# One table set for logarithm and exponential on ScalarE, and the recurrence's inverse roots as powers on GpSimd

## The reference

```python
# both layers: modulation
mod = (_silu(c) @ wmod).reshape(...)                  # sigmoid of 8 x 128 values, once
h = _layernorm(x) * (1 + ca) + sa                     # before each attention and each feed-forward
# layer 0: random-feature attention, feed-forward, and top-1 experts
qp = exp(xq - diag - max(xq)); kp = exp(xk - diag - max(xk over everything)); ...
x = layer_norm(video + attn, g2, be2); layer_norm(x + ff, g3, be3)
# layer 1: a recurrence over chunks of 64 tokens, for 16 heads of width 64
lr = sigmoid(xk_c @ theta + tb); eta = token_eta * lr / HD
Z1 = xk_c @ W + bb
std = sqrt(Z1.var(-1) + EPS); x_hat = (Z1 - mu) / std
grad_x = (HD * gxh - gxh.sum(-1) - x_hat * (gxh * x_hat).sum(-1)) / (HD * std)
Wn = W - (eta * xk_c).T @ grad_x                      # the next chunk needs Wn
Zq = xq_c @ Wn + bn
out = xq_c + g * (Zq - mu2) / sqrt(Zq.var(-1) + EPS) + be
# layer 1: the last feed-forward
r = sigmoid(xr @ W_r); out = r * (relu(xk @ W_k) ** 2 @ W_v)
```

## Time and profile before

| | |
|---|---|
| median of three runs | 1000.49 us (999.88 to 1000.78) |
| profiled execution, first to last instruction | 996.6 us, mean granted TensorE clock 0.973 |
| outside that span (median less span) | 3.9 us |
| busy: PE, DVE, ACT, POOL | 932.1, 792.1, 659.4, 332.9 us |
| ACT_TABLE_LOAD | 33 in the program's order, 1283 ns each |

### The profile page before, as it was taken

One profiled execution on the slowest core, in us unless ns is written; L12 is line 12 of the kernel. 1 busy time (PEld: TensorE's weight loads), 2 busy tenths in 40 slices (PEclk: granted clock), 3 DMA queues, 4 the chain that ended last, 5 costly groups with the idle time before them and its releaser, 6 DMA issues.

```text
span 996.6 us, 27072 instructions
## 1 busy us (share of the span) xinstructions
PE 932.1 (94%) x10930; PEld 710.6 (71%) x10930; DVE 792.1 (79%) x1953; ACT 659.4 (66%) x1246; POOL 332.9 (33%) x434
## 2 busy tenths in 40 slices
PE   6689899999999989899999999999999998999995
PEld 5566476777777776677778776677878766777772
DVE  3845549987989778997789869897888968888873
ACT  2363346689666576698756576699766567786772
POOL 1970002225241421224342322233442334455451
PEclk9689989999999999999999999999999999999998
DMA  9000010000000010000000010000000000000000
GB/s 330 14 2 1 1 43 2 2 2 2 3 1 2 13 44 1 2 2 2 2 13 1 12 33 12 1 3 2 3 12 2 10 14 13 1 4 12 3 2 21
DMA packets 15831, 16.03 MB, mean 16 GB/s; under 512 B 2013, under 2 KB 14301, under 8 KB 15325
## 3 DMA queue, kind: packets, MB, share of 16 engines
q1 hardware_dynamic: 15709, 14.31, 4.7%
HBM read 10.12 MB, written 2.10 MB: 12 GB/s over the span
## 4 chain that ended last, share of the span: by engine, by line
PE 65%; DVE 22%; ACT 6%; issue 3%; POOL 3%; DMA 1%; ACTq 0%; SPq 0%; DVEq 0%; POOLq 0%
PE ps L532 8%; PE ps L589 5%; PE ps L595 4%; PE ps L613 4%; PE ps L525 4%; PE ps L583 4%; PE ps L572 4%; PE ps L514 3%; PE ps L481 3%; PE ps L472 3%; PE ps L398 2%; PE ps L507 2%; DVE tmp L1111 2%; POOL gbase L1312 2%; DVE tmp L1116 2%
## 5 line engine op out<-in xcount | busy, mean ns | idle before, releaser
L1312 POOL TENSOR_TENSOR gbase<-zhat,gamma 128x512 f32<-128x512 f32 x64 | 81.7, 1276 | 320.6 <-DVE scl L1105 313.1
L1320 POOL TENSOR_TENSOR zq_sqq<-zq_sqq,qinv 128x512 f32<-128x512 f32 x64 | 67.9, 1063 | 260.9 <-DVE qinv L1128 254.7
L589 PEld LDWEIGHTS ps<-grad,k_sc 64*65 64x65 f32 x2048 | 67.2, 137 | 25.0 <-issue 22.9
L772 ACT COPY w_sb<-ps 65x1024 f32<-65x1024 f32 x66 | 66.4, 1007 | 24.7 <-PE ps L589 23.6
L532 PEld LDWEIGHTS ps<-w_sb,keys 65*64 65x64 f32 x2048 | 65.6, 138 | 21.7 <-issue 12.6
L532 PE MATMUL ps<-w_sb,keys 65*64 65x64 f32 x2048 | 73.1, 224 | 6.4 <-ACT keys L780 4.8
L589 PE MATMUL ps<-grad,k_sc 64*65 64x64 f32 x2048 | 74.9, 223 | 4.2 <-DVE grad L1122 4.0
L532 PEld LDWEIGHTS ps<-w_sb,queries 65*64 65x64 f32 x2048 | 65.1, 138 | 15.2 <-issue 10.0
L532 PE MATMUL ps<-w_sb,queries 65*64 65x64 f32 x2048 | 72.6, 224 | 2.7 <-issue 1.7
L595 PEld LDWEIGHTS ps<-h,pack_ttt 128*128 128x128 f32 x512 | 64.2, 195 | 11.3 <-issue 6.4
L595 PE MATMUL ps<-h,pack_ttt 128*128 128x128 f32 x512 | 70.7, 283 | 0.2 <-ACT k_tok L800 0.2
(11 more groups left out here) (244 smaller groups left out, 2346.7 us busy)
## 6 DMA issues: line engine op xcount, KB each, us to landing
x<-in_x SPq DMA_DIRECT2D x8, 256.0 KB, 3.5
xc<-x SPq DMA_DIRECT2D x16, 128.0 KB, 2.4
out_x<-xc SPq DMA_DIRECT2D x16, 128.0 KB, 2.4
pack_ttt<-in_ttt SPq DMA_DIRECT2D x1, 1216.0 KB
keys<-in_gam_bet_rows SPq DMA_DIRECT2D x1, 1024.0 KB
w_sb<-in_compose SPq DMA_DIRECT2D x1, 1024.0 KB, 9.3
zq_sqq<-in_wmod SPq DMA_DIRECT2D x1, 768.0 KB, 4.9
pack_expert<-in_expert SPq DMA_DIRECT2D x1, 680.0 KB, 16.0
```

The source lines that it names most:

```text
L589: last = mm(bank[2 * f + c][0:C, h * HD:(h + 1) * HD], k_sc[64 * c:64 * c + 64, HH * f + h, :], grad[64 * c:64 * c + 64, h, :], start=Fals ...
L772: nc.scalar.copy(w_sb[:, f, :, :, :].rearrange("p b h d -> p (b h d)"), ps[0:C, 2 * f:2 * f + 2, :].rearrange("p a c -> p (a c)")).then_in ...
L1312: P.tensor_tensor(gbase[:, cols], zhat[:, cols], gamma2[:, cols], ALU.mult).then_inc(S["g_hat"], 1)
L1320: P.tensor_tensor(heads(zq_hat[:, cols]), heads(zq_hat[:, cols]), per_head(qinv[:, hs]), ALU.mult).then_inc(S["zq_ready"], 1)
```

## The change

All of ACT's functions now come from one set (natural logarithm and exponential, with Square, Relu, Identity and Copy), loaded once at the start.

- **Layer norms.** ACT computes exp(-0.5 * ln(var + eps)) in two instructions on 128 x 4 values, and DVE's reciprocal is gone.
- **The recurrence's roots.** ACT has no part in them. POOL adds the epsilon (`zbase`, `qbase`) and raises to the power -0.5 (`zinv`, `qinv`), in a second instruction that waits for the first. DVE's two reciprocals per slot are gone. POOL's new letter `v` is the first root, and its `y` begins with the second.
- **Sigmoids.** They become 1 / (1 + exp(-x)): for the modulation and `eta`, DVE bounds the value, ACT takes the exponential, and DVE adds one and takes the reciprocal. For `r`, DVE bounds it out of PSUM (128 x 512), and ACT takes Exp, Ln and Exp again, each waiting for the one before; this stands in `MIX_OUT` instead of `MIX_IN`.
- **New order strings and banks** for all engines.

```diff
-    "DVE": ("111110001001001100111111000000111110011000001100r1001azbca0z0bcea1z1yazbecy0bc0a1zee1yay0bcz1bcaze11yebaycz111bc00aze1"
+    "DVE": ("1110110010001001101101101100010110111010000011000r01az1bca0z0bca1ez1azbec0bc1a0ez1ea0bzc1bcaz10e1bae1z1cbc01e0azb10c0a"
...
+            nc.scalar.preload_act_table_set("natural_log_exp_and_others")
             loaded(act, "mod")
-            nc.scalar.activation(s_sig[:, :, :], cT, ACT.Sigmoid).then_inc(act_set, 1)
...
+            def inverse_root(src, log, dst, sem, scale=1.0, eps=LN_EPS):
+
+                nc.scalar.activation(log, src, ACT.Ln, bias=eps, scale=scale).then_inc(S["logged"], 1)
+                logs[0] += 1
+                act.wait_ge(S["logged"], logs[0])
+                nc.scalar.activation(dst, log, ACT.Exp, scale=-0.5).then_inc(sem, 1)
...
-                elif what == "v":
-                    act.wait_ge(S["z_var"], g + 1)
-                    nc.scalar.activation(zstd[:, hs], ssum[:, hs], ACT.Sqrt, bias=TTT_EPS * HD).then_inc(S["z_std"], 1)
...
-                    src = filled(act, f"r_{n}")
-                    nc.scalar.activation(r_sb, src, ACT.Sigmoid).then_inc(drained(f"r_{n}"), 1)
+                elif step == MIX_OUT:
+                    ready(act, f"r_{n}")
+                    nc.scalar.activation(r_sb, r_sb, ACT.Exp, scale=-1.0).then_inc(S["r_step"], 1)
+                    act.wait_ge(S["r_step"], 2 * n + 1)
+                    nc.scalar.activation(r_sb, r_sb, ACT.Ln, bias=1.0).then_inc(S["r_step"], 1)
+                    act.wait_ge(S["r_step"], 2 * n + 2)
+                    nc.scalar.activation(r_sb, r_sb, ACT.Exp, scale=-1.0).then_inc(S["r_done"], 1)
...
             loaded(dve, "mod")
+            link0(V.tensor_scalar(s_sig[:, :, :], cT, SIG_LEAST, None, ALU.max))
             dve.wait_ge(act_set, 1)
+            link0(V.tensor_scalar(s_sig[:, :, :], s_sig[:, :, :], 1.0, None, ALU.add))
+            link0(V.reciprocal(s_sig[:, :, :], s_sig[:, :, :]))
...
                 elif what == "z":
-                    dve.wait_ge(S["z_std"], g + 1)
-                    link(V.reciprocal(zinv[:, hs], zstd[:, hs]))
+                    dve.wait_ge(S["z_inv"], g + 1)
...
-                elif what == "y":
-                    dve.wait_ge(S["zq_std"], g + 1)
-                    V.reciprocal(qinv[:, hs], qstd[:, hs]).then_inc(S["zq_inv"], 1)
...
-                if what == "z":
+                if what == "v":
+                    pool.wait_ge(S["z_var"], g + 1)
+                    if g >= 2:
+                        pool.wait_ge(S["scale_ready"], g - 1)
+                    P.tensor_scalar(zbase[:, hs], ssum[:, hs], TTT_EPS * HD, None, ALU.add).then_inc(S["z_base"], 1)
+                    pool.wait_ge(S["z_base"], g + 1)
+                    P.tensor_tensor(zinv[:, hs], zbase[:, hs], minus_half[:, :], ALU.pow).then_inc(S["z_inv"], 1)
+                elif what == "z":
...
                 elif what == "y":
+                    pool.wait_ge(S["zq_var"], g + 1)
+                    P.tensor_scalar(qbase[:, hs], qsum[:, hs], 1.0 / HD, TTT_EPS, ALU.mult, ALU.add).then_inc(S["zq_base"], 1)
+                    pool.wait_ge(S["zq_base"], g + 1)
+                    P.tensor_tensor(qinv[:, hs], qbase[:, hs], minus_half[:, :], ALU.pow).then_inc(S["zq_inv"], 1)
```

More of the change, by code:

```diff
@@ L96 @@
[L96 to L103, removed]
@@ L236, in build @@
         sq, tmp = sb("sq", [128, HALF]), sb("tmp", [128, HALF])
-        ssum, zstd, zinv, scl = (sb(n, [128, H]) for n in ("ssum", "zstd", "zinv", "scl"))
+        ssum, zbase, zinv, scl = (sb(n, [128, H]) for n in ("ssum", "zbase", "zinv", "scl"))
         zhat, gbase = (sb(n, [128, HW]) for n in ("zhat", "gbase"))
@@ L240, in build @@
         grad = sb("grad", [128, HH, HD])
-        qsum, qstd, qinv = (sb(n, [128, H]) for n in ("qsum", "qstd", "qinv"))
+        minus_half = sb("minus_half", [128, HH])
+        qsum, qbase, qinv = (sb(n, [128, H]) for n in ("qsum", "qbase", "qinv"))
         att1 = sb("att1", [128, 2, D])
@@ L680, in _ @@
         def _(act):
+            nc.scalar.preload_act_table_set("natural_log_exp_and_others")
             loaded(act, "mod")
-            nc.scalar.activation(s_sig[:, :, :], cT, ACT.Sigmoid).then_inc(act_set, 1)
-            def root(name, src, dst, u=None, scale=1.0, eps=LN_EPS):
-                key = name if u is None else f"{name}_{u}"
-                nc.scalar.activation(dst, src, ACT.Sqrt, bias=eps, scale=scale).then_inc(S[key], 1)
+            act.wait_ge(set_step, 1)
+            nc.scalar.activation(s_sig[:, :, :], s_sig[:, :, :], ACT.Exp, scale=-1.0).then_inc(act_set, 1)
+            logs = [0]
+            def inverse_root(src, log, dst, sem, scale=1.0, eps=LN_EPS):
[3 more added lines that the diff above has]
+                nc.scalar.activation(dst, log, ACT.Exp, scale=-0.5).then_inc(sem, 1)
             for u in range(2):
                 act.wait_ge(S[f"ln1_var_{u}"], 1)
-                root("ln1_std", L[u]["mv"][:, :, 1], L[u]["std"][:, :], u)
+                inverse_root(L[u]["mv"][:, :, 1], L[u]["log"][:, :], L[u]["inv"][:, :], S[f"ln1_inv_{u}"])
             loaded(act, "attn")
@@ L782, in start @@
             def start(p):
-                ready(act, f"rate_{p}")
-                nc.scalar.activation(eta[:, :, :], eta[:, :, :], ACT.Sigmoid).then_inc(S["rate_sig"], 1)
+                act.wait_ge(S["rate_bounded"], p + 1)
+                nc.scalar.activation(eta[:, :, :], eta[:, :, :], ACT.Exp, scale=-1.0).then_inc(S["rate_sig"], 1)
                 src = filled(act, f"g_att_{p}")
@@ L821, in slot @@
                     nc.scalar.copy(zq_hat[:, cols], src).then_inc(drained(f"zq_{g}"), 1)
-                elif what == "w":
-                    act.wait_ge(S["zq_var"], g + 1)
-                    nc.scalar.activation(qstd[:, hs], qsum[:, hs], ACT.Sqrt, bias=TTT_EPS, scale=1.0 / HD).then_inc(S["zq_std"], 1)
                 elif what == "f":
@@ L839, in mixing @@
                     act.wait_ge(S["ln6_var"], n + 1)
-                    nc.scalar.activation(std6[:, :], mv6[:, :, 1], ACT.Sqrt, bias=LN_EPS).then_inc(S["ln6_std"], 1)
+                    inverse_root(mv6[:, :, 1], log6[:, :], inv6[:, :], S["ln6_inv"])
                     if half == 0:
```

98 lines of the change are left out of this document (55 added, 43 removed).

## The result

The changed kernel takes **1163.57 us** (1162.29 to 1164.93 in four runs) against 1000.63 us of the kernel before beside it: a ratio of 1.168, 95% interval 1.160 to 1.176. It is 163 us slower; the forecast was 996.4 us, with a range to 1008.

What follows compares the result with a forecast made beforehand. PE was taken as the bound, busy 932.1 of 996.6 us. Terms -4.3 loads, -1.0 clock, -3.0 DVE, +0.7 and -1.6 head, +0.3 tail, +4.8 power sum to -4.1: 992.5, or 996.4 us with 3.9 around it; range 987 to 1008.

Steps and rivals of the forecast that it cites:

- P has no row: POOL's power on 128 x 8, between 0.19 and 1.28 us, taken at 0.40: +0.37 per slot, +4.8 us in all.
- the power is slow: Rival, chance 0.22: POOL's power takes up to 1.28 us or POOL is kept waiting; 1007 us, deciding from 0.71 on.
- 13 of 16 slots, and 0 in the earlier pairs: Only 13 last-pair slots pay for v's power, +4.8 us; layer-0 work on PE and DVE covers it in earlier pairs.
- my own formula: Last pair's loss from v's power: 13 slots x (P - 0.03) us, where P is one power's duration.
- The second root has a slot's slack: Query's root in POOL's y has a slot's slack before zT is wanted, so it adds no time.
- DVE's lighter work, -3.0: Reciprocals leave DVE; in three stretches where it is 94% busy this was worth up to 4.5 us, taken at 3.0.
- The head: Program's start: Q_SHIFT matmuls fill PE's 4.55 us gap and DVE's 1.61 us wait goes, -1.6; s_sig's extra steps +0.7.
- The tail: After the last r matmuls, DVE's bound and three activations replace the sigmoid: end at 991.3 instead of about 991.0, +0.3.
- The loads: Four ACT table loads on the chain, ahead of activations other than r's sigmoid, disappear: 4.34 us, counted as -4.3.
- the clock: A load at 368.6 us leaves PE nearly empty, with clock 0.54 behind it; two us at half clock, -1.0.
- DVE near 765, ACT near 612, POOL near 410: Busy times in us that the profile after the change was expected to show for the three engines.
- The shared read port: Skill's warning that GpSimd and VectorE share an SBUF read port, cited under the slow-power rival (chance 0.22), without its own time.

Runs made afterwards that it cites:

- both cheap: Changed kernel with both recurrence-root powers on POOL replaced by a subtraction of the same 128 x 8 shape: 1037.8 us (1.039).
- no roots: Recurrence's two roots left out, zinv and qinv set to zero once: 1030.9 us from the changed kernel, 1005.7 us from the kernel before.
- experiment 6: Changed kernel and kernel before without the recurrence's roots (1030.9 and 1005.7 us), and changed kernel with each power on 4 of 8 columns (1126.6); stage marks compared.
- v's power alone: Changed kernel with only the query root's power (y) replaced by a 128 x 8 subtraction, the power between ssum and zhat kept: 1116.9 us (1.119).
- cheap roots: Kernel before's orders, banks and tables, with both recurrence roots on POOL and a 128 x 8 subtraction in place of each power: 1021.4 us (1.020).
- y's alone: Changed kernel with only v's power (between ssum and zhat) replaced by a 128 x 8 subtraction, the query root's power kept: 1079.6 us (1.078).
- the new head alone: Kernel before with the changed kernel's order of the first 48 items on PE, ACT and DVE and its first 84 banks: 993.9 us (0.995).
- experiment 8: Kernels without roots, POOL's gbase and zq products cut to 8 columns: 996.0 us new orders, 995.0 old; slow DVE operations counted in the changed kernel's trace.

## Why the prediction was wrong, point by point

Measured terms of the 163 us: the powers' price over a cheap operation 126, the way through GpSimd 7 (new orders, within the intervals) to 16 (old orders; both cheap against no roots), the new orders 25 without roots, the rest (before against no roots with old orders) about 5 us, hardly more than the spread. With powers the orders cost 48 to 60, so part of the 126 is theirs as well: under the old orders the powers cost 94.

- **The price of the power: the step that failed first.** "P has no row", bounded by 0.19 and 1.28 and taken at 0.40; it is 1.68. The upper bound was the costliest operation that POOL did, on the argument that it ran over 64 times as many elements. A multiplication's price says nothing of a power's: per element they differ nearly eightyfold. The rival "the power is slow" had the right sign and decided at 0.71, but it too stopped at 1.28.
- **"13 of 16 slots, and 0 in the earlier pairs": the step that failed by more.** At 1.68 my own formula gives 13 x 1.65 = 21 us, and 13 x 1.46 = 19 against the cheap operation. By the marks of experiment 6, in single profiled runs (from mark to mark, in us):

| | pair 0's slots | pair 1's | pair 2's | the last pair's |
|---|---|---|---|---|
| both cheap | 209.5 | 240.0 | 246.4 | 216.8 |
| v's power alone | 226.5 | 257.8 | 264.7 | 242.9 |
| both powers | 240.1 | 268.2 | 273.7 | 257.6 |

  v's power costs 26 us in the last pair, where the formula was not far off, and 17, 18 and 18 in the three before, where I had put 0; both powers cost 41 there and 86 in the three. Of DVE's 57 waits for v's power 41 lie ahead of the last pair. So layer 0's work doesn't cover the longer answer: a slot with layer 0 beside it pays 1.1 of the 1.46 us. That each engine's list is in order, so that the item that waits holds up the layer-0 work behind it, is how I explain this; no run tests it. PE's 94% in a window of pair 1 or 2 read as cover. Even a short way costs something: under the old orders cheap roots against none, some 0.6 us a slot, lose 4, 1, 5 and 8 us in the four stretches.
- **"The second root has a slot's slack": wrong.** 42 to 47 us in the changed kernel, 26 us in the kernel before. POOL had room by its busy share, but PE waits for `zq_sqq`, which "a slot's slack" ruled out: 20.4 us, against 3.2 with y cheap. ACT's wait for `k_sc` (45.4 us) is mostly v's: it is 39.1 with v's power alone and 25.4 with y's alone.
- **The orders: counted as a gain of 1.6 in the head and as nothing elsewhere.** I costed the places that I looked at and took the rest as sound. The middle pairs lost 8.5 and 16 us with the same code under both orders.
- **DVE's lighter work, -3.0.** No run shows it. Under the old orders, taking both roots and their reciprocals out gave no gain at all (ratio 1.005, 1.000 to 1.009).
- **The head: right in sign, mis-sized.** -1.6 was forecast for the order (-0.9 with the +0.7 of `s_sig`), and the new head alone measured -4.9. PE's wait of 4.55 us for `kmx` shrank to 1.32 (the first row below), and DVE's 1.61 is gone, as forecast. "PE's next wait, for stream 0's maximum, stays, and with it the low clock behind it" held too: the wait is 4.50 us (the second row; 2.93 before, at 48.88), and the clock is 0.50 from 44 to 52 us. But it comes 5.3 us earlier. What I left out lies on both sides of the place that I costed: with the new head alone DVE's first work on `QKV` (`v<-ps`, line 978) starts at 19.69 instead of 21.80 us, and the low clock behind the first wait is mostly gone. PE after, in order of time:

```profile
32.29 0.27 PE L406 MATMUL ps<-pack_attn,kmx 128*16 128x128 f32 x1 [1.32 <-DVE kmx L1012]
...
43.61 0.37 PE L406 MATMUL ps<-pack_attn,kmx 128*16 128x128 f32 x1 [4.50 <-DVE kmx L1012]
```

  The window between these two waits, before and then after, columns as in the earlier trace rows:

```profile
36.00:44.00 8.00, 8.00 (x35) 6.35 (x36) 6.13 (x13) 0.00 (x0) 7.67 (x14) 0.50 0.00 0
```

```profile
36.00:44.00 8.00, 3.50 (x18) 2.27 (x15) 7.22 (x14) 4.23 (x8) 7.67 (x14) 0.71 0.00 0
```

  Before, PE worked through these 8 us at 0.50, the lower of its two levels (1.2 of 2.4 GHz); after, it issues 18 matmuls there instead of 35, is partly idle, waiting for DVE's second `kmx`, and has 0.71 on the mean.
- **The tail: +0.3.** From the end of the `r` matmuls to the next step it is 2.79 us after and was 2.40, so +0.4.
- **The loads: -4.3, and the clock: -1.0.** One load is left, at the start, as said. The mean clock went the other way, to 0.931, with PE's waits. No gain was seen: one table set against the old tables is equal within the intervals under the new orders, and under the old ones with roots on ACT 1.5% slower than before. The gain of 0.5% that I forecast is about what those intervals leave open.
- **DVE near 765, ACT near 612, POOL near 410.** ACT 622.5 is near. DVE has 153 fewer instructions and is busy 16 us more, and its four operations on two SBUF tiles take 204 us instead of 185, with means of 746 to 829 ns where their medians are 692 to 694. Against the 765 I had also left out the bound, addition and reciprocal for `eta`, 5.6 us. POOL, cheap, shows 412.6, so the miss there is the power alone.
- **The shared read port.** I put this rule of the Trainium skill (Perfetto Trace Analysis, on optimizing Vector and Scalar operations), that moving work between GpSimd and VectorE may not help, beside a rival and gave it no time. The rows agree that POOL's work slows DVE's: `grad` at 1.36 us beside POOL's product, median 0.69, and the 78 slow operations of experiment 8. They don't show a port. With the products narrowed, the gap of 25 us went down to 1. It was no part of the forecast's sum.

## What to carry to other kernels

An operation with no row in the trace has no upper bound from other operations' rows: measure it alone, by size, before building on it. Added latency inside a loop that crosses engines can be paid in nearly every turn, even where another engine looks 94% busy; here 1.46 us cost 1.1 in a slot with other work beside it, and 1.6 in one without. When a change bundles an order of work with an operation, run the order alone: its first 48 items were worth 5 us, and the whole of it still cost 25.

## What the runs showed of the hardware

- GpSimd's power on 128 partitions takes 0.4 us and 0.16 us for each fp32 element of a partition: 0.57 us for 1, 1.65 for 8, 82.15 for 512. A multiplication takes 0.20, 0.21 and 1.26 us.
- VectorE's multiplications and subtractions of two SBUF tiles of 128 x 512 take 0.69 us alone and at most 1.26 to 1.58 us, by the instruction, beside a wide multiplication or addition on GpSimd. A power on GpSimd, 1.66 us long on 8 elements a partition, doesn't slow them (45 cases). The slots' reductions (650 to 687 ns) and instructions that read PSUM (653 to 693 ns) keep their time. The same 64 instructions, in the same code, cost 741 or 840 ns on average, by the order of work alone.
